# First unit of three attention layers: row maxima in twice as many parts, and a new merge order

## The chip, the cores and the metric

The kernel runs on one core of a Trainium2 chip. The metric is the device time of one execution, in microseconds (us); less is better. The core has a matrix engine (PE in the tables, TensorE), a vector engine (DVE, VectorE), an activation engine (ACT, ScalarE), a general engine (POOL, GpSimd) and SyncE (SP), which here only issues DMAs. Each runs its own instruction stream in order and waits for the others on semaphores.

## What is computed

Eight sequences of 128 tokens and 256 channels go through four layers. Each adds a gated cross attention and then a gated feed-forward block to x. The four attentions differ in heads and shapes, the softmax core is the same:

```
x = x + tanh(g_xattn[0]) * L0_xattn(layernorm(x), ctx)      # 16 heads of 8, 256 x 256 scores, per sequence
x = x + tanh(g_ffn[0])   * L0_ffn(layernorm(x))             # 8 experts, top 1 with capacity
x = x + tanh(g_xattn[1]) * L1_xattn(layernorm(x), ctx, ctx) # 8 heads of 16, 256 x 256 scores, per sequence
x = x + tanh(g_ffn[1])   * L1_ffn(layernorm(x))             # gate, up, down
x = x + tanh(g_xattn[2]) * L2_xattn(layernorm(x), ctx, mask)# 16 heads of 16, scores clipped at 50: no maxima
x = x + tanh(g_ffn[2])   * L2_ffn(layernorm(x))             # 16 experts, top 2, and a shared one
x = x + tanh(g_xattn[3]) * L3_xattn(layernorm(x), ctx)      # 16 heads of 16, all 1024 tokens against 1024 keys,
                                                            # q, k, v and the probabilities rounded to 8 bits
x = x + tanh(g_ffn[3])   * L3_ffn(layernorm(x))             # 4 experts, top 1

scores = q k^T * scale
attn = softmax(scores)          # exp(scores - row maximum) / sum
out = attn v
```

## The kernel before

The program is made in two steps. `plan()` writes one list of steps for the whole kernel; then each engine's program is that list walked from front to back, an engine emitting its own share of each step. So the order of the list is the order on every engine, the DMA queue of SyncE included.

An attention works in **units**: one sequence in the first three layers (8 units), two sequences (256 queries) in the last (4 units). A unit has these steps:

- the **front**: normalise, project (`fq`, `fk`), split fp32 into bf16 parts (`split`, on POOL), store them to DRAM (`store`) and load them back packed (`packs`);
- the **maxima tiles** (`smax`): PE makes scores of 128 queries in one PSUM bank (lines 1338 in the last layer, 1344 in the first two), DVE reduces each bank to row maxima (lines 1929 and 1933). A unit has 16 tiles in the first layer, 8 in the second, 64 in the last. They take turns in three banks (`psB`), which the projections and transposes use too;
- per **part** of the heads: the **negation** (`negsplit`, DVE lines 1943 to 1960: the maxima of the part are negated and split into two or three bf16 numbers), and the **turn** (`negmax`): PE transposes them (line 1354), ACT copies them out of PSUM (line 1659), and SyncE issues two or three DMAs that put them as extra rows under the queries (line 1180, `whole<-nmT`). With these rows a score matmul gives score minus maximum at once. The first two layers have one part a unit, the last has two;
- the **body**: for each group of 4 heads and each 128 keys a **score group** (`st`, 4 matmuls, line 1374), the exponential on ACT (line 1675), in the last layer a rounding on POOL (`round`, line 2342), and the **value group** (`pv`, lines 1406, or 1408 and 1418), one to three score groups later; after each group of heads `onorm` (line 1425, DVE lines 1976 and 1979). The first layer has 8 score groups a unit, the second 4, the last 32. The first score group of a part waits for that part's extra rows;
- the **end**: transposes, output projection, the update of x.

What sets the order is a merge: every stream of steps has a start and an end time in units, counted from the layer's start, and `merge` sorts all steps by them. The times stand in `TIMES`, one dict a layer. The body of a unit runs beside the maxima tiles of the next.

```
            if A.has_max:
                begin = u + at["max"] if u else at["max_first"]
                step = (u + at["max_end"] - begin) / A.parts
                for tiles, split, turn in maxes(units[u]):
                    begin += step
                    streams += [(tiles, begin - step, begin), ([split], begin, begin),
```

## Time and profile before

| | |
|---|---|
| median of 3 runs | 1189.02 us (1188.04 to 1189.3) |
| profiled execution, its own time | 1187.16 us |
| its span in the trace | 1185.4 us |
| busy share: PE, DVE, ACT, POOL | 80%, 56%, 37%, 32% |
| first layer's attention | about 8 to 185 us |
| second layer's attention | about 312 to 395 us |
| last layer's attention | about 714 to 1000 us |

The shares are means over stages of very different kind, so the argument goes by stretches. A row of the timeline tells the start, the duration, the engine and line, what is written and read, and how many instructions of that kind ran back to back; in square brackets how long the engine had been idle before, and who released it. A row of the windows tells the length of the stretch, the busy time of PE, PEld (weight loads), DVE, ACT and POOL in it with the number of instructions, and then the TensorE clock that was granted, where 1.00 is 2.4 GHz and 0.50 is 1.2 GHz, the DMA engines' share and GB/s.

### The profile page before, as it was taken

The page shows a single profiled execution, that of the slowest core. Times are in us where ns is not written, and L with a number is a line of the kernel's source. Part 1 is how long each engine was busy: PE and PEld are TensorE (multiplying, and loading weights), DVE is VectorE, ACT ScalarE, POOL GpSimd, SP SyncE. Part 2 cuts the span into 40 slices and gives each one's busy share as a digit, 9 for nine tenths or more (in the row PEclk, how much of TensorE's full clock was granted, in tenths as well). Part 3 has the DMA queues.
Part 4 walks back from the last instruction along what each step waited for, and adds up shares of the span by engine and source line. Part 5 has one row for each costly group of instructions (what it writes and reads, how often), then busy time and mean ns, then how long its engine had stood idle before and what let it go on. Part 6 is the DMA issues. An engine that isn't in the chain of part 4 may idle for free.

```text
span 1185.4 us, 18900 instructions
## 1 busy us (share of the span) xinstructions
PE 945.1 (80%) x6620; PEld 558.2 (47%) x6620; DVE 660.6 (56%) x1574; ACT 438.3 (37%) x722; POOL 383.5 (32%) x515
## 2 busy tenths in 40 slices
PE   3899985798299999777379726999989997199993
PEld 1455544687044456554247612344434444156662
DVE  5678753462679334777623358787887852211111
ACT  1366662111056313443014300466546575021220
POOL 5233204332631003442050061356555565200002
PEclk9999996989589999996589956699999999599997
DMA  6434524684543004542327530101210002700002
GB/s 183 122 102 146 175 82 186 187 291 153 125 113 83 1 1 121 173 95 67 142 102 227 170 95 15 41 2 42 108 42 2 2 3 108 267 21 23 14 14 80
DMA packets 112700, 116.32 MB, mean 98 GB/s; under 512 B 58824, under 2 KB 102408, under 8 KB 109576
## 3 DMA queue, kind: packets, MB, share of 16 engines
q1 hardware_dynamic: 101760, 96.62, 26.5%
q10 hardware_dynamic: 7776, 10.10, 2.6%
q0 software_dynamic: 3072, 8.39, 2.3%
q8 instruction: 56, 0.92, 0.3%
q14 instruction: 36, 0.29, 0.1%
HBM read 88.17 MB, written 30.67 MB: 100 GB/s over the span
## 4 chain that ended last, share of the span: by engine, by line
PE 47%; DVE 14%; DMA 7%; issue 7%; POOL 6%; ACT 2%; SPq 1%; POOLq 0%; ACTq 0%; DVEq 0%
PE psT L1523 7%; PE psT L1223 5%; PE psT L1374 5%; PE psB L1338 4%; DVE mxp L1929 4%; PE psB L1223 4%; PE psO L1418 3%; PE psB L1537 3%; PE psT L1486 2%; PE psB L1588 2%; PE psO L1408 2%; DMA scr_k_high<-sk 1%; PE psO L1406 1%; POOL scr_sorted L2354 1%; PE psB L1564 1%
## 5 line engine op out<-in xcount | busy, mean ns | idle before, releaser
L1929 DVE TENSOR_REDUCE mxp<-psB 128x1 f32<-128x512 f32 x256 | 163.7, 684 | 37.5 <-PE psB L1338 36.7
L1374 PE MATMUL psT<-whole 99*128 99x256 bf16 (+2 forms) x1024 | 153.1, 275 | 10.0 <-issue 9.0
L1933 DVE TENSOR_REDUCE mxp<-psB 128x2 f32<-128x512 f32 x192 | 123.5, 684 | 31.6 <-PE psB L1344 31.2
L1675 ACT ACTIVATE Pt<-psT,ln 128x1024 f32<-128x1024 f32 x96 | 106.7, 1114 | 63.8 <-PE psT L1374 62.7
L1374 PEld LDWEIGHTS psT<-whole 99*128 99x128 bf16 (+2 forms) x1024 | 96.5, 102 | 54.1 <-issue 21.5
L1675 ACT ACTIVATE Pt<-psT 128x1024 f32<-128x1024 f32 x96 | 98.1, 1024 | 58.3 <-PE psT L1374 56.6
L1338 PE MATMUL psB<-whole 96*128 96x512 bf16 x256 | 96.2, 427 | 24.3 <-DMA whole<-scr_q 13.9
L2283 POOL TENSOR_TENSOR rstd<-vare,cst 128x1 f32<-128x1 f32 x64 | 35.8, 562 | 231.3 <-DVE vare L1836 231.0
L1344 PE MATMUL psB<-whole 96*128 96x256 bf16 x384 | 78.0, 306 | 36.0 <-DMA whole<-scr_q 20.3
L1523 PE MATMUL psT<-whole,qf 128*128 x176 | 82.3, 612 | 0.6 <-ACT qf L1729 0.6
L2342 POOL TENSOR_SCALAR nb_t<-Pt 128x1024 f16<-128x1024 f32 x64 | 67.2, 1051 | 39.5 <-ACT Pt L1675 37.4
L2204 DVE TENSOR_TENSOR Pt<-psT,Pt 128x512 f32<-128x512 f32 x22 | 15.2, 691 | 100.3 <-ACT Pt L1735 100.3
L1344 PEld LDWEIGHTS psB<-whole 96*128 96x128 bf16 x384 | 30.7, 105 | 83.8 <-issue 34.8
L1406 PE MATMUL psO<-Pt,whole 128*32 128x256 f32 x768 | 62.9, 401 | 3.8 <-ACT Pt L1675 2.8
L1338 PEld LDWEIGHTS psB<-whole 96*128 96x128 bf16 x256 | 20.6, 100 | 89.2 <-issue 39.7
L1223 PE MATMUL psT<-xn_t,whole 128*128 128x512 f32 (+1 forms) x128 | 59.2, 614 | 0.0
L1418 PE MATMUL psO<-Pt,cst 128*32 128x256 f32 x768 | 59.2, 385 | 0.0
L2373 POOL DMA_INDIRECT xn_t<-scr_sorted_out,idx x8 | 7.7, 958 | 140.4 <-DMA scr_sorted_out<-xn 138.3
L1231 PE MATMUL psB<-cst,xn 128*128 128x128 f32 x96 | 23.3, 330 | 33.1 <-DVE xn L1769 32.2
L1523 PEld LDWEIGHTS psT<-whole,qf 128*128 128x128 f32 x176 | 32.8, 197 | 34.2 <-issue 34.2
L1425 PE MATMUL psB<-cst,Oe 128*128 128x128 f32 x160 | 37.8, 304 | 13.7 <-ACT Oe L1683 8.6
L1669 ACT ACTIVATE Pt<-nb_t,att_b,att 128x512 f32<-128x512 f32 x32 | 26.0, 813 | 48.9 <-DVEq L1969 48.6
(323 smaller groups left out, 1743.8 us busy)
## 6 DMA issues: line engine op xcount, KB each, us to landing
whole<-in_w SPq DMA_DIRECT2D x32, 512.0 KB, 5.2
whole<-in_w SPq DMA_DIRECT2D x5, 3072.0 KB, 10.3
xn<-scr_sorted ACTq DMA_DIRECT2D x42, 128.0 KB, 2.2
scr_q<-sq SPq DMA_DIRECT2D x48, 96.0 KB, 2.2
whole<-scr_q SPq DMA_DIRECT2D x24, 192.0 KB
whole<-scr_k SPq DMA_DIRECT2D x24, 192.0 KB, 3.5
scr_sorted_out<-xn SPq DMA_DIRECT2D x31, 128.0 KB, 2.4
scr_k<-sk SPq DMA_DIRECT2D x32, 96.0 KB, 1.9
```

The lines of the kernel that those rows point to most:

```text
L1223: ins = pe.matmul(dst, lhsT=lhs(kd), rhs=rhs(kd), start=(kd == 0), stop=(kd == halves - 1))
L1338: ins = pe.matmul(dst, lhsT=q_at[:, h * A.T + s.tc * P:h * A.T + (s.tc + 1) * P], rhs=k_at[:, h * NT + half * 512:h * NT + (half + 1) * 51 ...
L1344: ins = pe.matmul(dst[:, i * 256:(i + 1) * 256], lhsT=q_at[:, h * A.T + s.tc * P:h * A.T + (s.tc + 1) * P], rhs=k_at[:, h * A.T:(h + 1) * ...
L1374: ins = pe.matmul(psT[:, s.n % 2, i * A.T:(i + 1) * A.T], lhsT=k_at[:, h * kw + s.c * P:h * kw + (s.c + 1) * P], rhs=q_at[:, h * A.T:(h + ...
L1406: ins = pe.matmul(dst, lhsT=VA[:, u.g % 3, s.c * A.H + h, :], rhs=pr, start=first, stop=last)
L1418: ins = pe.matmul(dst, lhsT=const("sumsel"), rhs=pr, start=False, stop=last)
L1425: ins = pe.transpose(dst[:, tc * P:(tc + 1) * P], Oe[:, s.o % 2, tc * P:(tc + 1) * P], ident)
L1523: ins = pe.matmul(psT[:, s.n % 2, k * 512:(k + 1) * 512], lhsT=xeT[:, s.i % 2, kd, :], rhs=whole[:, bass.ds(s.un.k * SLOTW + at, 512)], st ...
L1675: act.activation(p_slot(A, s.p)[:, 0:4 * A.T], psT[:, s.n % 2, 0:4 * A.T], ACT.Exp, bias=bias, scale=scale).then_inc(T_used[s.n % 2], 1)
L1929: dve.tensor_reduce(mxp[:, s.un.g % 2, at:at + 1], psB[:, s.n % BANKS, :], AX.X, ALU.max).then_inc(bank_used[s.n % BANKS], 1)
L1933: dve.tensor_reduce(mxp[:, s.un.g % 2, at:at + 2], psB[:, s.n % BANKS, :].rearrange("p (h n) -> p h n", h=2), AX.X, ALU.max).then_inc(bank ...
L2342: pool.tensor_scalar(n_slot(s.p)[:, 0:w], p_slot(s.A, s.p)[:, 0:w], 1.0, OFFSET, ALU.mult, ALU.add).then_inc(rounded, 1)
```

## The change

It gives a unit its own number of parts: the first unit of each attention has 2 instead of 1 part (first and second layer) and 4 instead of 2 (last layer). The other units keep theirs. The times of the merge become separate for the first unit (`first_end`, `first_body`) and for the start of the second one's maxima (`max_second`), and the other times are new too. The first unit's body starts earlier in the order, while its later parts' maxima are still being made. No arithmetic changes but the order of the maxima tiles.

```diff
+FIRST_PARTS = (2, 2, 1, 4)
...
 TIMES = [
-    dict(front=0.339, store=0.638, packs=0.793, max=1.019, max_end=1.817, neg=1.926, body=2.312, end=3.927, start=0.17, span=1.026, max_first=1.418),
-    dict(front=0.315, store=0.667, packs=1.608, max=1.871, max_end=2.713, neg=2.846, body=3.334, end=5.364, start=0, span=0.958, max_first=2.13),
...
-    dict(front=0, fronts=[0.0, 0.005, 0.01, 0.02, 0.03, 0.04, 0.045, 0.045, 0.045, 0.045, 0.045, 0.058, 0.06, 0.079], rest=[0.0, 0.02, 0.06, 0.08, 0.11, 0.13, 0.15, 0.18, 0.21, 0.24, 0.27, 0.33, 0.34, 0.35], store=0.42, packs=0.43, max=0.909, max_end=1.919, neg=1.973, body=1.639, end=3.415, start=0, span=1.008, max_first=1.026)]
+    dict(front=0.327, store=0.638, packs=0.793, max=1.019, max_end=1.831, neg=2.01, body=2.312, end=3.957, start=0.17, span=1.026, max_first=1.484, first_end=2.214, first_body=2.177, max_second=1.253),
+    dict(front=0.315, store=0.667, packs=1.608, max=1.871, max_end=2.551, neg=2.846, body=3.334, end=5.364, start=0.047, span=0.911, max_first=2.13, first_end=2.545, first_body=3.087, max_second=1.871),
...
+    dict(front=0, fronts=[0.0, 0.005, 0.01, 0.02, 0.03, 0.04, 0.045, 0.045, 0.045, 0.045, 0.045, 0.058, 0.06, 0.079], rest=[0.0, 0.02, 0.06, 0.08, 0.11, 0.13, 0.15, 0.18, 0.21, 0.24, 0.27, 0.33, 0.34, 0.372], store=0.408, packs=0.43, max=0.942, max_end=1.936, neg=2.001, body=1.639, end=3.334, start=0, span=1.008, max_first=1.026, first_end=1.85, first_body=1.36, max_second=0.75)]
...
+            r.parts = FIRST_PARTS[A.layer] if u == 0 else A.parts
...
-                begin = u + at["max"] if u else at["max_first"]
-                step = (u + at["max_end"] - begin) / A.parts
+                begin = at["max_first"] if u == 0 else 1 + at["max_second"] if u == 1 else u + at["max"]
+                end = at["first_end"] if u == 0 else u + at["max_end"]
+                step = (end - begin) / units[u].parts
...
-            streams += [(body(units[u]), u + at["body"], body_end), (finish(units[u]), body_end + at["start"], u + at["end"]),
+            streams += [(body(units[u]), u + at["body"] if u else at["first_body"], body_end), (finish(units[u]), body_end + at["start"], u + at["end"]),
```

On PE at the head of the last layer's attention, from the middle of the first unit's maxima on (L1338 a maxima tile, L1354 the turn of a part, L1374 a score group), there stood before:

```order
L1338 MATMUL psB<-whole 128x512 x13
L1354 MATMUL psB<-ident,npt 24x128 x2
L1338 MATMUL psB<-whole 128x512 x9
L1374 MATMUL psT<-whole 128x256 x4
L1338 MATMUL psB<-whole 128x512 x2
L1374 MATMUL psT<-whole 128x256 x4
L1338 MATMUL psB<-whole 128x512 x2
L1374 MATMUL psT<-whole 128x256 x4
```

and now (the lines are three higher):

```order
L1341 MATMUL psB<-whole 128x512 x13
L1357 MATMUL psB<-ident,npt 12x128 x2
L1341 MATMUL psB<-whole 128x512 x3
L1278 MATMUL psB<-cst,tmp 128x128 x4
L1341 MATMUL psB<-whole 128x512 x3
L1377 MATMUL psT<-whole 128x256 x4
L1341 MATMUL psB<-whole 128x512 x3
L1377 MATMUL psT<-whole 128x256 x4
```

The first score group had 45 maxima tiles ahead of it and has 27; three instead of two tiles stand between score groups after it.

On PE in the second layer, from the last value group of a unit to the turn of the next but one, as it repeats from unit to unit (L1344 x2 is one maxima tile, L1231 a transpose for the feed-forward block, L1425 `onorm`, L1406 a value group), before:

```order
L1406 MATMUL psO<-Pt,whole 32x256 x4
L1231 MATMUL psB<-cst,xn 128x128 x2
L1344 MATMUL psB<-whole 128x256 x2
L1425 MATMUL psB<-cst,Oe 128x128 x2
L1344 MATMUL psB<-whole 128x256 x4
L1374 MATMUL psT<-whole 128x256 x4
L1344 MATMUL psB<-whole 128x256 x4
L1374 MATMUL psT<-whole 128x256 x4
L1406 MATMUL psO<-Pt,whole 32x256 x4
L1344 MATMUL psB<-whole 128x256 x2
L1374 MATMUL psT<-whole 128x256 x4
L1406 MATMUL psO<-Pt,whole 32x256 x4
```

and now:

```order
L1409 MATMUL psO<-Pt,whole 32x256 x4
L1234 MATMUL psB<-cst,xn 128x128 x2
L1347 MATMUL psB<-whole 128x256 x4
L1428 MATMUL psB<-cst,Oe 128x128 x2
L1347 MATMUL psB<-whole 128x256 x4
L1377 MATMUL psT<-whole 128x256 x4
L1347 MATMUL psB<-whole 128x256 x4
L1377 MATMUL psT<-whole 128x256 x4
L1409 MATMUL psO<-Pt,whole 32x256 x4
L1377 MATMUL psT<-whole 128x256 x4
L1409 MATMUL psO<-Pt,whole 32x256 x4
```

The tile that stood behind the first value group has moved ahead of the first score group, so that four tiles of that unit precede the score group instead of three.

On PE at the end of the first layer, around the turn of the last unit (L1354), before:

```order
L1406 MATMUL psO<-Pt,whole 32x256 x4
L1354 MATMUL psB<-ident,npt 32x128 x2
L1374 MATMUL psT<-whole 128x256 x4
L1406 MATMUL psO<-Pt,whole 32x256 x4
L1374 MATMUL psT<-whole 128x256 x4
```

and now:

```order
L1409 MATMUL psO<-Pt,whole 32x256 x4
L1377 MATMUL psT<-whole 128x256 x4
L1409 MATMUL psO<-Pt,whole 32x256 x4
L1357 MATMUL psB<-ident,npt 32x128 x2
L1377 MATMUL psT<-whole 128x256 x4
```

The turn comes one score group and one value group later.

## Rows read from the trace of the kernel before

**Rows 1.** The page's chain that ended last, share of the span by engine
```profile
PE 47%; DVE 14%; DMA 7%; issue 7%; POOL 6%; ACT 2%; SPq 1%; POOLq 0%; ACTq 0%; DVEq 0%
```

**Rows 2.** Windows of the last attention: length, busy time, clock, DMA share, GB/s
```profile
716.62:750.24 33.62, 27.33 (x61) 7.86 (x62) 31.25 (x59) 1.91 (x5) 3.70 (x5) 0.60 0.12 36
750.24:776.24 26.00, 25.88 (x225) 11.65 (x224) 19.52 (x37) 17.24 (x17) 13.59 (x13) 0.82 0.01 2
776.24:810.90 34.66, 31.85 (x338) 15.72 (x336) 28.38 (x52) 21.40 (x25) 21.64 (x21) 1.00 0.13 35
810.90:816.85 5.95, 5.79 (x63) 2.07 (x62) 5.32 (x9) 1.57 (x3) 2.09 (x2) 1.00 0.04 8
```

**Rows 3.** Timeline of DVE at the head of the last attention
```profile
737.08 5.47 DVE L1929 TENSOR_REDUCE mxp<-psB 128x1 f32<-128x512 f32 x9 [0.42 <-PE psB L1338]
742.58 0.18 DVE L1943 TENSOR_REDUCE nm<-mxp 128x16 f32<-128x32 f32 x1
...
743.52 8.06 DVE L1929 TENSOR_REDUCE mxp<-psB 128x1 f32<-128x512 f32 x13
```

**Rows 4.** Timeline of PE in the last attention
```profile
750.24 1.06 PE L1374 MATMUL psT<-whole 99*128 99x256 bf16 x4
751.09 1.06 PE L1338 MATMUL psB<-whole 96*128 96x512 bf16 x2
751.95 1.06 PE L1374 MATMUL psT<-whole 99*128 99x256 bf16 x4
...
758.53 1.00 PE L1374 MATMUL psT<-whole 99*128 99x256 bf16 x4
...
765.57 0.60 PE L1374 MATMUL psT<-whole 99*128 99x256 bf16 x4
...
767.20 0.60 PE L1374 MATMUL psT<-whole 99*128 99x256 bf16 x4
...
816.85 0.60 PE L1374 MATMUL psT<-whole 99*128 99x256 bf16 x4
```

**Rows 5.** Tile nm on DVE: duration in ns, least, median, greatest
```profile
L1952 DVE TENSOR_SCALAR npt<-nm x8: 174/186/823, 742.8 to 963.0; 128x16 bf16<-128x16 f32 x8
...
L1959 DVE CAST npt<-nm x8: 174/175/904, 743.2 to 963.6; 128x16 bf16<-128x16 f32 x8
```

**Rows 6.** Timeline of the second attention's repeating unit: PE, then DVE, then ACT
```profile
362.77 0.39 PE L1344 MATMUL psB<-whole 96*128 96x256 bf16 x2 [0.20 <-DVE mxp L1933]
363.00 0.60 PE L1374 MATMUL psT<-whole 98*128 98x256 bf16 x4
...
364.77 0.64 PE L1406 MATMUL psO<-Pt,whole 128*32 128x256 f32 x8
...
363.07 2.47 DVE L1933 TENSOR_REDUCE mxp<-psB 128x2 f32<-128x512 f32 x4
...
363.70 2.06 ACT L1675 ACTIVATE Pt<-psT 128x1024 f32<-128x1024 f32 x2 [1.65 <-PE psT L1374]
```

**Rows 7.** Timeline of the second attention's head: PE, then DVE
```profile
325.48 1.04 PE L1374 MATMUL psT<-whole 98*128 98x256 bf16 x4 [0.53 <-DMA whole<-nmT]
...
317.74 0.48 DVE L2220 SCALAR_TENSOR_TENSOR x<-xn_t,r,x 128x256 f32<-128x256 f32 x1 [0.27 <-DMA xn_t<-scr_expert_out,idx]
```

**Rows 8.** Timeline of the first attention's head: PE, then SP's queue
```profile
40.64 1.06 PE L1374 MATMUL psT<-whole 98*128 98x256 bf16 x4
...
55.00 0.38 PE L1344 MATMUL psB<-whole 96*128 96x256 bf16 x2 [3.25 <-issue]
...
45.31 0.89 SPq L1115 DMA_DIRECT2D scr_k<-sk  x2
```

**Rows 9.** Timeline of the first attention's end: PE, then SP's queue
```profile
160.84 0.28 PE L1354 MATMUL psB<-ident,npt 128*32 128x128 bf16 x2
...
165.44 0.60 PE L1374 MATMUL psT<-whole 98*128 98x256 bf16 x4
...
161.63 1.16 SPq L1180 DMA_DIRECT2D whole<-nmT  x2
```

More of the change, by code:

```diff
@@ L69, in __init__ @@
         self.b0 = b0
-        self.k_packed = self.k_packed_before = None
+        self.k_packed = self.k_packed_before = self.parts = None
 P = 128
@@ L145 @@
 TIMES = [
-    dict(front=0.339, store=0.638, packs=0.793, max=1.019, max_end=1.817, neg=1.926, body=2.312, end=3.927, start=0.17, span=1.026, max_first=1.418),
-    dict(front=0.315, store=0.667, packs=1.608, max=1.871, max_end=2.713, neg=2.846, body=3.334, end=5.364, start=0, span=0.958, max_first=2.13),
-    dict(front=0.368, fronts=[-0.15, 0.1, 0.278, 0.262, 0.45], store=0.58, packs=0.684, body=1.604, end=3.227, start=0.084, span=1.053),
-    dict(front=0, fronts=[0.0, 0.005, 0.01, 0.02, 0.03, 0.04, 0.045, 0.045, 0.045, 0.045, 0.045, 0.058, 0.06, 0.079], rest=[0.0, 0.02, 0.06, 0.08, 0.11, 0.13, 0.15, 0.18, 0.21, 0.24, 0.27, 0.33, 0.34, 0.35], store=0.42, packs=0.43, max=0.909, max_end=1.919, neg=1.973, body=1.639, end=3.415, start=0, span=1.008, max_first=1.026)]
+    dict(front=0.327, store=0.638, packs=0.793, max=1.019, max_end=1.831, neg=2.01, body=2.312, end=3.957, start=0.17, span=1.026, max_first=1.484, first_end=2.214, first_body=2.177, max_second=1.253),
+    dict(front=0.315, store=0.667, packs=1.608, max=1.871, max_end=2.551, neg=2.846, body=3.334, end=5.364, start=0.047, span=0.911, max_first=2.13, first_end=2.545, first_body=3.087, max_second=1.871),
+    dict(front=0.368, fronts=[-0.15, 0.1, 0.278, 0.262, 0.45], store=0.58, packs=0.684, body=1.604, end=3.227, start=0.084, span=1.053, first_body=1.604),
+    dict(front=0, fronts=[0.0, 0.005, 0.01, 0.02, 0.03, 0.04, 0.045, 0.045, 0.045, 0.045, 0.045, 0.058, 0.06, 0.079], rest=[0.0, 0.02, 0.06, 0.08, 0.11, 0.13, 0.15, 0.18, 0.21, 0.24, 0.27, 0.33, 0.34, 0.372], store=0.408, packs=0.43, max=0.942, max_end=1.936, neg=2.001, body=1.639, end=3.334, start=0, span=1.008, max_first=1.026, first_end=1.85, first_body=1.36, max_second=0.75)]
 def plan():
@@ L347, in maxes @@
             r.neg = []
-            per = A.H * A.NC * P // 512 // A.parts
-            for part in range(A.parts):
+            per = A.H * A.NC * P // 512 // r.parts
+            for part in range(r.parts):
                 tiles = []
@@ L375, in st @@
                 s = add("st", A=A, un=r, g=g, c=c, first=(i == 0), n=take("T"), p=take("P"))
-                if A.has_max and c == 0 and g % (A.G // A.parts) == 0:
-                    s.neg = r.neg[g * A.parts // A.G]
+                if A.has_max and c == 0 and g % (A.G // r.parts) == 0:
+                    s.neg = r.neg[g * r.parts // A.G]
                 s.clip = take("clip") if A.layer == 2 else None
@@ L1178, in _ @@
                         r = A.rows + p3
-                        HP = A.H // A.parts
+                        HP = A.H // s.un.parts
                         sp.dma_start(QP[r:r + 1, s.un.g % 3, s.j * HP * A.T:(s.j + 1) * HP * A.T],
@@ L1351, in _ @@
                     pe.wait_ge(neg_split, s.i + 1)
-                    w = A.lows * A.H // A.parts
+                    w = A.lows * A.H // s.un.parts
                     for tc in range(A.TC):
@@ L1657, in _ @@
                         act.wait_ge(neg_in[s.i % 2], neg_after[s.i - 2])
-                    w = A.lows * A.H // A.parts
+                    w = A.lows * A.H // s.un.parts
                     act.activation(nmT[0:w, s.i % 2, 0:A.T], m_slot(s.m).bitcast(BF16)[0:w, 0:A.T],
@@ L1936, in _ @@
                 elif s.kind == "negsplit":
-                    A, HP = s.A, s.A.H // s.A.parts
+                    A, HP = s.A, s.A.H // s.un.parts
                     w = A.TC * HP
                     turn(dve, bank_used, s.last_S)
-                    mx = mxp[:, s.un.g % 2, 0:w]
+                    src = mxp[:, s.un.g % 2, 0:A.TC * A.H].rearrange("p (t h) -> p t h", t=A.TC)[:, :, s.j * HP:(s.j + 1) * HP]
                     if A.layer == 3:
@@ L1944, in _ @@
                                                halves_[:, :, s.j * HP:(s.j + 1) * HP, :], AX.X, ALU.max))
-                        mx = nm[:, 1, 0:w]
+                        src = nm[:, 1, 0:w].rearrange("p (t h) -> p t h", t=A.TC)
                     if s.m_prev2 is not None:
@@ L1949, in _ @@
                     part = npt[:, s.i % 2, 0:A.lows * w].rearrange("p (t c h) -> p c t h", t=A.TC, c=A.lows)
-                    src = mx.rearrange("p (t h) -> p t h", t=A.TC)
                     left = nm[:, 0, 0:w].rearrange("p (t h) -> p t h", t=A.TC)
```

## The prediction

> **What bounds the kernel now.** I read the page's chain first: it runs 47% on TensorE, 14% on VectorE, 7% each on DMA and issue [rows 1]. So the kernel is bound by TensorE where it is dense and by somebody else at the heads of stages. Then the windows of the last attention, cut at its first maxima tile (716.62 us), its first score group (750.24), group 14 after it (776.24), the last of the first unit's groups that have maxima tiles between them (810.90), and the second unit's first score group (816.85). In the first window VectorE is busy 31.25 of 33.62 us and TensorE 27.33, at a granted clock of 0.60; in the second TensorE is busy 25.88 of 26.00; in the third 31.85 of 34.66, at clock 1.00, with VectorE at 28.38 [rows 2]. So ahead of the first score group VectorE's reductions set the time and everything that a score group feeds stands idle; behind it TensorE does. The change moves work over that border, in the one direction that can pay: TensorE's groups go into the stretch where it waits. For the other two attentions I read the timeline at the head, in one repeating unit and at the end.
>
> **Last attention, head.** A maxima tile costs VectorE 5.47 / 9 = 0.61 us [rows 3]. Of the first unit's tiles 45 preceded the first score group, now 27: 18 × 0.61 = 11.0 us earlier, at 739.3. Those 18 tiles aren't gone. From the first maxima tile to the second unit's first score group there were 111 tiles and are 113; I lay them out by the same three stretches. Groups 1 to 14 had 28 tiles beside them and have 43; the next 17 had 30 and have 33; the piece behind them had 8 and has 10 (less the groups, 45 + 28 + 30 + 8 before, 27 + 43 + 33 + 10 now).
>
> *Stretch two* becomes VectorE's: 43 × 0.61 = 26.2 us. Three negations lie in it. One costs 0.94 us when nothing disturbs it, from 742.58 to the next reduction at 743.52 [rows 3]. Its small instructions take 0.19 and 0.18 us in the median, but up to 0.82 and 0.90 [rows 5]; two such make 0.94 + 0.64 + 0.72 = 2.3. I take 1.3, nearer the undisturbed one because the medians are, so 3.9. The group's normalisation adds 0.5 (estimate, two small instructions beside those). While the clock is at 0.5 TensorE can be the later of the two: a score group then costs 0.85 (750.24 to 751.09) and a tile 0.43 (0.86 for two, to 751.95); four intervals with two tiles each, and one value group, took 8.29 [rows 4]. With 11 tiles instead of 8 and a turn that is 8.29 + 3 × 0.43 + about 0.2 to 0.4 = 9.7, against 11 × 0.61 + 1.0 = 7.7 on VectorE. Of these 2.0 us the three banks' backlog covers part; I add 1.0. Sum 26.2 + 3.9 + 0.5 + 1.0 = **31.6** (29.5 with negations at 0.94 and no wait; 35.9 with them at 2.3 and the wait at 2.0, and 0.3 more for the turn of each part) for 26.00 before.
>
> *Stretch three*: 34.66 before. Three more tiles cost VectorE 3 × 0.61 = 1.8, and TensorE 3 × 0.22 = 0.7 (half of the 0.43). TensorE was busy 31.85 there and VectorE 28.38 [rows 2]; both have room, so between nothing and 1.8; I take 1.3: **36.0**. *Tail*: 5.95 with VectorE busy 5.32 of it [rows 2]; two more tiles, 0.4 to 1.2: **6.5**.
>
> Sum 739.3 + 31.6 + 36.0 + 6.5 = 813.4 for 816.85 [rows 4], **-3.4 us**. Low end 739.3 + 29.5 + 34.7 + 6.4 = 809.9 (-6.9), high end 739.3 + 35.9 + 36.5 + 7.2 = 818.9 (+2.0). From the second unit on the order differs by single tiles, and TensorE is dense, so the shift reaches the end whole. I cost at nothing: two more turns there (two small transposes each, on TensorE under half a score group's 0.85 us [rows 4]), because VectorE is the later one; and SyncE's six more DMAs. Two such issues take 1.16 us [rows 9], so six are 3.5 us of a queue whose engines carry 1% in that stretch [rows 2]. If the second unit's loads, which stand ahead of the later parts' turns, came late, those 3.5 us would be added to the wait.
>
> The Trainium skill, "SBUF — State Buffer", section "Who interferes with whom", says that VectorE's copies, casts and scalar operations and GpSimd's work lock each other out for a whole instruction, while reductions don't take part. The trace agrees: the two forms of row 5 are the ones with the long maxima, 823 and 904 ns [rows 5]. By that rule a negation that falls beside roundings on GpSimd costs the 2.3 us of my upper bound; were all three to, the sum would be 3 us worse, +0.8 in all.
>
> **Second attention.** Head: the turns of both parts stand one behind the other and behind all 8 tiles of the unit, so little of the split can be used. VectorE besides waits until 317.74 for the combine of the layer before [rows 7]. The first score group comes at 325.48 behind its rows' DMA [rows 7]; it can be at most about 1.1 us earlier (two tiles' reductions of 0.6), but the second unit's maxima set the next step. Taken as **0** (-1.1 to 0.5). Repeating unit: the first score group (363.00) is released by reductions that take 2.47 / 4 = 0.62 us each [rows 6], and has one tile more ahead: +0.6. The tile no longer stands behind the first value group, so the later groups close up, but no nearer than ScalarE's exponential allows, 2.06 / 2 = 1.03 each, idle 1.65 us before the first [rows 6]: -0.35, half of a reduction. So +0.25 in each of the five intervals with this pattern, and -0.3 in the last one, where no tile is added ahead: **+1.0**. The ends are 0 (ScalarE's idle time hides all of it) and +2.0 (no closing up in three of the five).
>
> **First attention.** Head: the first body is dense from 40.64; the first wait is 3.25 us before 55.00, for the third unit's loads [rows 8]. They hang on the store at 45.31, and that on the projections of keys, which now have four reductions fewer ahead, up to 2.4 us. But the second part's row DMAs now stand in SyncE's queue ahead of that store, 1.16 us [rows 9] before its 0.89 [rows 8]. Half of what is left, **-0.7** (-1.6 to 0). End: the last unit's turn (160.84) moves behind one score group and one value group, 1.1 us; its rows are issued at 161.63 for 1.16 us and are needed at 165.44 [rows 9]. There the slack after issue is 2.65 us, which the landing mostly uses, as the 0.53 us wait for such rows elsewhere shows [rows 7]: **+0.9** (0 to +1.2). Together +0.2.
>
> **Sum.** -3.4 + 1.0 + 0.2 = -2.2 us. Against the profiled execution, 1187.16, this is 1185.0; against the median of 1189.02 it is **1186.8**. The profiled execution lies 1.9 us under that median, so I shift both alike. 0.2% is 2.4 us, about what a measurement of this kernel can tell from no change; the forecast lies just inside.
>
> **Rivals.**
> *VectorE never waits.* Negations run undisturbed, the half-clock stretch is covered, and the second attention's added tile hides in ScalarE's 1.65 us: -6.9 + 0 - 0.7 = -7.6, 1181.4. For it: VectorE was busy 31.25 of 33.62 us when it alone set the time [rows 2]. Against it: rows 5's maxima. 0.28.
> *The head's gain is given back.* VectorE becomes the bound of the whole first body, its added negations fall beside GpSimd's roundings, and score groups wait behind three tiles each at half clock: +2.0 + 1.0 + 0.2 = +3.2, 1192.2. Its place is stretch two; it decides once that stretch takes over 34 us (26.00 before, + 11.0 gained ahead, - 1.9 for the two stretches behind, - 1.2 for the other attentions). For it: GpSimd is busy 13.59 of 26.00 us there [rows 2], about half, so a negation often meets one. Against: the median is the undisturbed value. 0.15.
> *The clock doesn't rise.* TensorE ran at 0.60 while it waited for reductions and at 0.82 and 1.00 when dense [rows 2], and in the stretch it now waits again. A group with two tiles and a value group takes 767.20 - 765.57 = 1.63 us at full clock [rows 4], with a third tile 1.85, while VectorE sets 31.6 / 14 = 2.26. At half clock it is 0.85 + 3 × 0.43 and 1.2 for the value group (estimate: the 8.29 us of four intervals less 4 × 1.71 leaves 1.45 [rows 4], a wait included), 3.3. So every group that stays at half clock beyond my first four costs 1.0, two undo the forecast, and all ten make +10.4: -2.2 + 10.4 = +8.2, 1197.2. 0.07. [...]
>
> **How the numbers follow.** Forecast 0.50, of which 0.15 falls beyond 0.2% faster and 0.35 within; with 0.28 that is faster 0.43, same 0.35, and slower 0.15 + 0.07 = 0.22. The range reaches from the first rival's 1181.4 to the slower one's 1192.2; outside lie the clock rival and what overshoots the other ends.
>
> **What would show it.** The first score group of the last attention at about 22.7 us behind the first maxima tile instead of 33.6; 14 groups later VectorE busy over 90% of some 31 us, TensorE with short waits on reductions; the second unit's first score group 3 us nearer to the first maxima tile; a clock of 0.7 or more in stretch two. In the second attention each unit 0.25 us longer, in the first attention's end a wait of under 1 us for `nmT` rows. I am wrong if stretch two takes over 34 us, or if the shift is not there at the second unit's first group.

## The result, and the profile after

| | before | changed |
|---|---|---|
| median of 20 runs each | 1186.24 us (1182.36 to 1192.88) | 1179.07 us (1172.09 to 1188.04) |
| ratio | | 0.9941, 95% interval 0.9922 to 0.9959 |
| profiled execution, its own time | 1187.16 us | 1172.09 us |

The change makes the kernel 0.59% faster, some 7 us (0.41% to 0.78%), where I had forecast 2.2 us. The profiled execution of the changed kernel is the fastest of its 20, 7 us under their median, so the 15 us between the two profiles are not the effect. What can be compared are stretches that came out alike in many profiles. The table takes the starts of score groups from the timelines. Its "first maxima tile" is the tile's start on TensorE (714.02 us before, 706.99 now); the prediction and the windows below count from VectorE's first reduction of one, 2.6 to 2.7 us later (716.62 and 709.70). "Old" and "new" say whether the stretch has the order of before or of the change; the experiments below gave 14 more profiles. A value without a bracket is that of the two main profiles.

| stretch | old order | new order |
|---|---|---|
| start to last score group of first attention | 175.35 (174.23 to 176.59, 8 profiles) | 171.53 (171.53 to 174.88, 7 profiles) |
| second attention, second unit's first group to the last | 54.99 (54.36 to 55.22, 12 profiles) | 55.24 (55.23 to 55.24, 4 profiles) |
| last attention, first maxima tile to first group | 36.22 | 25.83 |
| 14 groups from there | 26.00 | 35.78 |
| 17 more | 34.66 | 34.73 |
| to the second unit's first group | 5.95 | 6.18 |
| second unit's body | 68.55 (68.54 to 68.61, 4 profiles) | 63.56 (63.56 to 63.58 in 3 profiles, 65.22 in a fourth) |
| third unit's body | 61.30 | 59.96 |
| fourth, to its last group | 46.38 | 46.93 |

The profiles counted for the first row have one order in the first attention. Stretches in between that no edit touches (the feed-forward blocks with their gathers, and the third attention) scatter by 1 to 7 us each between profiles, and 6.4 of the 15 us between the two main ones stand there.

The page's chain of the changed kernel, and the windows of its last attention; the first four rows stand for those of [rows 2]:

```profile
PE 48%; DVE 13%; DMA 7%; issue 6%; POOL 6%; ACT 2%; SPq 1%; POOLq 0%; ACTq 0%; DVEq 0%
```
```profile
709.70:732.82 23.12, 16.27 (x42) 5.75 (x43) 20.40 (x42) 1.91 (x5) 0.60 (x2) 0.65 0.00 1
732.82:768.60 35.78, 30.80 (x244) 12.74 (x243) 30.76 (x57) 17.67 (x18) 16.69 (x17) 0.86 0.12 35
768.60:803.33 34.73, 32.79 (x342) 16.07 (x341) 29.50 (x61) 21.59 (x25) 20.43 (x21) 1.00 0.01 1
803.33:809.51 6.18, 5.99 (x65) 2.14 (x64) 5.80 (x11) 1.55 (x3) 2.98 (x3) 1.00 0.65 179
809.51:873.07 63.56, 60.62 (x633) 29.56 (x631) 53.70 (x104) 39.67 (x45) 38.35 (x38) 1.00 0.21 72
873.07:933.03 59.96, 59.08 (x629) 28.57 (x628) 49.81 (x97) 38.85 (x43) 34.52 (x34) 1.00 0.01 2
```

The second unit's and the third unit's body of the kernel before, which the prediction didn't look at, and a piece out of the second unit's:

```profile
816.85:885.40 68.55, 62.62 (x633) 29.99 (x632) 56.58 (x106) 39.40 (x44) 38.41 (x38) 0.98 0.19 65
885.40:946.70 61.30, 59.19 (x629) 28.53 (x628) 48.86 (x97) 38.67 (x42) 34.57 (x34) 1.00 0.01 2
871.99:875.40 3.41, 3.41 (x26) 1.06 (x19) 1.56 (x3) 1.11 (x1) 2.85 (x4) 0.50 0.43 118
```

Three things are to be seen. The first score group comes 10.4 us nearer to the first maxima tile, and the next 14 groups take 9.8 us longer: of the head next to nothing stays. The second unit's body is 5.0 us shorter with as many instructions on TensorE (633); TensorE idled 68.55 - 62.62 = 5.9 us in it and idles 2.9. And the clock of that body went from 0.98 to 1.00. Before, it stood at 0.50 for 3.4 us from 871.99 on, which is some 1.7 us (half of 3.4, an estimate) of the 2.0 by which TensorE's busy time fell.

In the first 14 groups VectorE is busy 30.76 us, and I had summed 26.2 + 3.9 + 0.5 = 30.6. That it fits so well is partly luck: only two negations fall into this stretch, of 2.4 and 1.2 us (737.64 and 753.40), and the third comes at 769.09, behind its end. The other 5.0 us it waits for TensorE, for which I had set 1.0. The timelines of VectorE, of GpSimd and of TensorE show the place:

```profile
737.64 0.17 DVE L1946 TENSOR_REDUCE nm<-mxp 128x8 f32<-128x16 f32 x1
737.85 0.86 DVE L1954 TENSOR_SCALAR npt<-nm 128x8 bf16<-128x8 f32 x1
738.75 0.17 DVE L1959 SCALAR_TENSOR_TENSOR nm<-nm,npt 128x8 f32<-128x8 f32 x1
738.95 0.90 DVE L1961 CAST npt<-nm 128x8 bf16<-128x8 f32 x1
739.88 0.17 DVE L1962 TENSOR_TENSOR npt<-nm,npt 128x8 bf16<-128x8 f32 x1
...
743.94 0.69 DVE L1932 TENSOR_REDUCE mxp<-psB 128x1 f32<-128x512 f32 x1 [1.49 <-PE psB L1341]
...
746.94 3.73 DVE L1932 TENSOR_REDUCE mxp<-psB 128x1 f32<-128x512 f32 x6 [1.46 <-PE psB L1341]
```
```profile
737.64 2.18 POOL L2344 TENSOR_SCALAR nb_t<-Pt 128x1024 f16<-128x1024 f32 x2
```
```profile
740.71 0.61 PE L1341 MATMUL psB<-whole 96*128 96x512 bf16 x1 [2.65 <-DVE mxp L1932]
741.11 1.06 PE L1377 MATMUL psT<-whole 99*128 99x256 bf16 x4
...
744.54 1.06 PE L1377 MATMUL psT<-whole 99*128 99x256 bf16 x4
```

The windows on either side of the clock's fall:

```profile
736.00:739.40 3.40, 1.85 (x10) 0.67 (x7) 3.17 (x7) 2.38 (x3) 2.90 (x4) 1.00 0.40 118
739.40:746.20 6.80, 5.49 (x37) 2.06 (x37) 4.39 (x8) 1.99 (x3) 1.47 (x2) 0.50 0.38 116
```

The second part's negation meets two roundings and takes 2.4 us from its first instruction to the end of its last, instead of 1.0. TensorE's next tile needs a bank whose reduction stands behind this negation, so it waits 2.65 us. Within the wait its granted clock falls to 0.50, that is to 1.2 GHz, and stays there for 6.8 us (a score group takes 1.06 instead of 0.60). TensorE is now the later one itself, and VectorE waits twice 1.5 us. Each engine pays for the other's stall.

### The profile page after: what moved, and what is told of

The parts are those of the page before. It is cut to its first block, busy times and chain, and to the rows that moved or that the text cites. A ratio compares the mean times of both kernels' runs of the same rounds, so it can differ in the third digit from the quotient of the medians.

```text
span 1170.3 us, 18962 instructions
## 1 busy us (share of the span) xinstructions
PE 931.2 (80%) x6628; PEld 553.5 (47%) x6628; DVE 660.9 (56%) x1588; ACT 439.5 (38%) x726; POOL 382.9 (33%) x515
## 4 chain that ended last, share of the span: by engine, by line
PE 48%; DVE 13%; DMA 7%; issue 6%; POOL 6%; ACT 2%; SPq 1%; POOLq 0%; ACTq 0%; DVEq 0%
PE psT L1526 7%; PE psT L1226 6%; PE psT L1377 5%; PE psB L1341 4%; PE psB L1226 4%; PE psO L1421 4%; PE psB L1540 3%; DVE mxp L1932 3%; PE psT L1489 2%; PE psB L1591 2%; PE psO L1411 2%; PE psO L1409 1%; DVE mxp L1936 1%; POOL scr_sorted L2356 1%; PE psB L1567 1%
## 5 line engine op out<-in xcount | busy, mean ns | idle before, releaser
L1341 PE MATMUL psB<-whole 96*128 96x512 bf16 x256 | 90.1, 408 | 29.1 <-DVE mxp L1932 14.8
L1347 PE MATMUL psB<-whole 96*128 96x256 bf16 x384 | 75.4, 300 | 34.2 <-DMA whole<-scr_q 20.7
L1622 ACT ACTIVATE xn_t<-psB 128x256 f32<-128x256 f32 x48 | 18.2, 379 | 69.2 <-PE psB L1234 68.3
```

The lines of the kernel that those rows point to most:

```text
L1341: ins = pe.matmul(dst, lhsT=q_at[:, h * A.T + s.tc * P:h * A.T + (s.tc + 1) * P], rhs=k_at[:, h * NT + half * 512:h * NT + (half + 1) * 51 ...
L1347: ins = pe.matmul(dst[:, i * 256:(i + 1) * 256], lhsT=q_at[:, h * A.T + s.tc * P:h * A.T + (s.tc + 1) * P], rhs=k_at[:, h * A.T:(h + 1) * ...
```

## The experiments

All kernels are the changed one with some of its numbers put back. A layer "put back" has its old row of `TIMES`, with `first_end`, `first_body` and `max_second` equal to `max_end`, `body` and `max`, which gives the order of before. Ratios are to the kernel before; kernels without one had a single timed run.

**One layer at a time.**

```diff
-FIRST_PARTS = (2, 2, 1, 4)
+FIRST_PARTS = (2, 1, 1, 2)   # e1_l0: rows 2 and 4 of TIMES put back
+FIRST_PARTS = (1, 2, 1, 2)   # e2_l1: rows 1 and 4 put back
+FIRST_PARTS = (1, 1, 1, 4)   # e3_l3: rows 1 and 2 put back
```

> Only the first attention has the change; the other layers keep their old parts and times. If my prediction's working for this layer holds (head -0.7, end +0.9), the time is within 1 us of the kernel before. If the reading of the trace after holds (the third unit's loads land earlier, the wait of 3.25 us before its first maxima tile almost goes, and with it the drop of TensorE's clock behind it), this kernel is 3 to 4 us faster, and in the trace the third unit's first score group (index 8) comes 3 to 4 us earlier, and the last group of the layer still 3 to 4 us earlier.

Measured 0.9965 (0.9938 to 0.9992), some 4 us faster. Score group 8 stands at 57.64 instead of 61.70, the layer's last at 172.20 instead of 175.35. Groups are counted from 0 and a unit has eight, so group 8 is the second unit's first one, not the third's as the expectations for e1_l0 and e8_l0_head call it; the wait ahead of it is that for the third unit's loads.

> Only the second attention has the change. Prediction and the trace after agree: +0.2 us a unit, about +1 us in all between the second unit's first score group and the last one, -0.6 to -1 given back in the last unit; whole kernel 0 to 1.5 us slower. A rival is that the earlier first score group (split turn) pays 1 us and this layer is worth nothing.

Measured 0.9998 (0.9976 to 1.0019): nothing. From one unit's first group to the next it takes 8.97, 8.90, 8.89, 8.75 and 8.75 us instead of 8.52, 8.69, 8.69, 8.55 and 8.58, so +1.2 in five intervals, and 7.24 instead of 8.22 in the last one. The repeating unit, in the changed kernel, on TensorE and on ScalarE, for [rows 6]:

```profile
358.20 0.60 PE L1377 MATMUL psT<-whole 98*128 98x256 bf16 x4
...
359.98 0.64 PE L1409 MATMUL psO<-Pt,whole 128*32 128x256 f32 x8
```
```profile
358.90 2.06 ACT L1678 ACTIVATE Pt<-psT 128x1024 f32<-128x1024 f32 x2 [2.25 <-PE psT L1377]
```

The first value group still stands 1.8 us behind the first score group (1.77 before, 1.78 now), and ScalarE waits 2.25 instead of 1.65 us for that score group: the added tile is the 0.6 us.

> Only the last attention has the change. Prediction: first unit's head -3.4 us, nothing behind it. From the trace after: head -0.3 to -1 (half-clock stretch and negations beside GpSimd's rounding eat the 11 us), and 4 to 6 us in the second unit's body. If that second part was an accident of one execution, this kernel is only 0 to 2 us faster and its second body takes about 68 us as before; if it is due to the new order, the second body takes about 64 us and the kernel is 4 to 7 us faster.

Measured 0.9960 (0.9939 to 0.9982). The head takes 102.36 us to the second unit's first group (102.83 before), the second body 63.58: both as in the changed kernel, to 0.2 us. It was no accident.

**The last attention without the new first unit.**

```diff
-FIRST_PARTS = (2, 2, 1, 4)
+FIRST_PARTS = (1, 1, 1, 2)
-    first_end=1.85, first_body=1.36, max_second=0.75     # last row; rows 1 and 2 put back
+    first_end=1.919, first_body=1.639, max_second=0.909
```

> Only the last attention, and of it only the times that every unit uses (max, max_end, neg, store, end, rest); the first unit keeps two parts and its old head. If the gain in the second body comes from the steady order, it is here as well (second body 64 instead of 68 us, kernel 3 to 5 us faster). If the gain comes from the head, this kernel is within 1 us of the kernel before.

Measured 0.9964 (0.9938 to 0.9989), the same as e3_l3. The second body takes 64.90 us, the third 59.96, the fourth 46.91. From the first maxima tile to the layer's last group it is 272.96 us, with four parts in e3_l3 272.82. So nearly all of the last layer's gain is that of the times which all units share; the split of its first unit is worth 0.1 us in this pair. It has an effect in both directions: with it the second body is 1.3 us shorter (63.58), and the head 1.2 us longer (102.36 against 101.19).

**Which of these times.** Between the two bodies the traces differ at one conspicuous place. In the kernel before GpSimd's split of the next unit's queries (L2264 to L2267) stands in front of a rounding. The rounding ends at 871.51, and TensorE's value group starts at 871.61 after 1.78 us of idling; the row names no releaser, so that it waited for this rounding is inferred. Behind it TensorE runs slow. First GpSimd, then TensorE:

```profile
866.58 0.62 POOL L2264 TENSOR_SCALAR sq<-qf 128x512 bf16<-128x512 f32 x1
...
869.22 1.15 POOL L2267 TENSOR_TENSOR sq<-rem,sq 128x512 bf16<-128x512 f32 x1
870.47 1.04 POOL L2342 TENSOR_SCALAR nb_t<-Pt 128x1024 f16<-128x1024 f32 x1
```
```profile
871.61 0.29 PE L1408 MATMUL psO<-nb_t,whole 128*32 128x256 f16 x4 [1.78 <-issue]
...
872.88 1.06 PE L1374 MATMUL psT<-whole 99*128 99x256 bf16 x4
```

```diff
-    rest=[0.0, ..., 0.34, 0.35]     # last row as before, all rows put back
+    rest=[0.0, ..., 0.34, 0.372]    # e6_split: this alone
```

> The kernel before with one number changed: in the last layer the last entry of rest is 0.372 instead of 0.35. That moves one thing: in the second unit's body GpSimd's split of the queries (four instructions, 3.8 us) stands behind one more rounding; every other engine's order is the same. Theory: the split stood ahead of a rounding that TensorE's next value group needed; TensorE waited 1.8 us for it and then ran at half clock. Then the second body takes about 65 us instead of 68.6, and the whole kernel is 3 us faster. Rival: the gain in the second body comes from the maxima's new times (max, max_end, neg); then this kernel's second body still takes 68 us or more.

Measured 0.9983 (0.9964 to 1.0002), second body 68.38 us. My theory fell. The split now stands one rounding later, and a value group waits for the rounding behind it, with TensorE at half clock again (0.98 over the body, as before):

```profile
870.44 0.39 PE L1411 MATMUL psO<-whole 128*32 128x256 f16 x4 [1.56 <-POOL whole L2344]
```

> The last attention with the steady times of the change and the first unit's old head, as e4_l3_rest, but with the last entry of rest left at 0.35. If the place of the split is what counts, the second body takes 67 to 69 us here and the third stays at 60.0. If the maxima's times count, it takes about 65 us as in e4_l3_rest.

(e4_l3_rest with the last entry of `rest` at 0.35.) Second body 67.53, third 59.96, fourth 46.92 us, as expected if the split's place counts. Without the split's new place the second body gains 1.0, with it alone 0.2, with both 3.65: no sum of parts.

> The kernel before with two of the last layer's times changed: end 3.334 (a unit's finish and the next normalisation earlier) and the last entry of rest 0.372. My theory that the split's place alone makes the second body faster fell (68.4 us). New theory: GpSimd stands behind the normalisation's rstd, which waits for VectorE (3.99 us idle in the kernel before), and then meets the split; only both moved together help. Then the second body takes 65 to 66 us here. If the maxima's times are needed too, it stays at 67 us or more.

(The kernel before with `end` 3.334 and `rest` 0.372.) Second body 65.83, third 60.45 us.

> The kernel before with the last layer's max, max_end, neg and the last entry of rest changed, end left at 3.415. By the theory of rstd and split together the second body stays at 67 us or more; if the maxima's times and the split are what counts, it takes about 65 us as in e4_l3_rest. The third body's 1.34 us (61.30 to 59.96) and the fourth's loss of 0.54 us (46.38 to 46.92) are there if they come from the maxima's times, and not if they come from end.

(The kernel before with `max` 0.942, `max_end` 1.936, `neg` 2.001 and `rest` 0.372.) Second body 66.38, third 60.77, fourth 46.81 us. e11's body lies within the 65 to 66 us expected, but the theory behind it said that the maxima's times do nothing, and e12 lies between its two outcomes. With the split moved, either of the other two brings 2.0 to 2.6 us more than e6_split, and 0.85 (e11) or 0.53 us (e12) of the third body's 1.34. Neither `end` nor the maxima's times were changed alone, and `store` (0.42 to 0.408) in none of the pairs. The windows of the second body show what goes with its time:

| kernel | body, us | TensorE busy | idle | granted clock | longest wait |
|---|---|---|---|---|---|
| before | 68.55 | 62.62 | 5.9 | 0.98 | 1.78, value group |
| e6_split | 68.38 | 62.67 | 5.7 | 0.98 | 1.56, value group |
| e7_no_split | 67.53 | 63.24 | 4.3 | 0.97 | 1.54, tile |
| e12_max_split | 66.38 | 61.43 | 5.0 | 1.00 | 1.29, value group |
| e11_end_split | 65.83 | 62.42 | 3.4 | 1.00 | 0.86, tile |
| e4_l3_rest | 64.90 | 61.54 | 3.4 | 1.00 | 1.54, tile |
| changed | 63.56 | 60.62 | 2.9 | 1.00 | 1.54, tile |

The idle time falls from 5.9 to 2.9 us, and the three slowest are those whose clock fell. So what is shown is that the order does it, not which wait: that stays open. A wait of 1.54 us on a tile was followed by a slow score group in e7 and in e10 below, and not in e4 and the changed kernel, so its length alone doesn't decide. Why TensorE is busy for 62.42 us in e11 at full clock is open.

**The first attention's first unit alone.**

```diff
-TIMES[0]: max_first=1.418
+TIMES[0]: max_first=1.484, first_end=2.214, first_body=2.177, max_second=1.253   # e8_l0_head, 2 parts; all else put back
```

> Only the first attention, and of it only the first unit (two parts, max_first, first_end, first_body, max_second); the times that all units use stay old. If the first layer's gain comes from its head, the third unit's first score group is 3 to 4 us earlier than in the kernel before (61.7 to 62.1 us there, once 59.9), and the layer's last score group 4 us earlier. If it takes the moved fronts and turns as well, it is 1 to 2 us earlier only.

Group 8 at 59.97, last group at 173.29 us: 1.7 and 2.1 us earlier than in the kernel before, or 1.0 and 2.3 against the means of the eight old profiles (60.93 and 175.58). That is nearer to the second outcome. The head brings at least this part; whether the rest is the order or where the loads landed can't be told from one profile.

**What the collision of negation and rounding costs.** Two ways to rewrite VectorE's instructions in the last layer, with the same results (-2x + x is -x; `zero` is a bf16 tile of zeros):

```diff
-link(dve.tensor_scalar(part[:, 0], src, -1.0, None, ALU.mult))
+link(dve.scalar_tensor_tensor(out=part[:, 0], in0=src, scalar=-2.0, in1=src, op0=ALU.mult, op1=ALU.add))    # e9
+link(dve.scalar_tensor_tensor(out=part[:, 0], in0=src, scalar=-1.0, in1=zero, op0=ALU.mult, op1=ALU.add))   # e10
...
-link(dve.tensor_copy(part[:, 1], left))
+link(dve.scalar_tensor_tensor(out=part[:, 1], in0=left, scalar=1.0, in1=left, op0=ALU.mult, op1=ALU.max))   # e9
+link(dve.scalar_tensor_tensor(out=part[:, 1], in0=left, scalar=1.0, in1=zero, op0=ALU.mult, op1=ALU.add))   # e10
```

> The changed kernel, but the last layer's negation uses scalar_tensor_tensor for its first and fourth instruction instead of tensor_scalar and the cast; the numbers are the same. In the changed kernel these two took 0.86 and 0.90 us beside GpSimd's rounding in the second part's negation, and TensorE stood 2.65 us behind it and then ran at 1.2 GHz. If those two instructions wait for GpSimd because of their form, they take under 0.25 us now, the wait falls to about 1 us, and the second unit's first score group is 1.5 to 4 us earlier than in the changed kernel (102.4 us behind the first maxima tile there). If every VectorE instruction waits for GpSimd, nothing changes.

> The changed kernel, but the last layer's negation takes for its first and fourth instruction a scalar_tensor_tensor that adds a bf16 tile of zeros, so that one input is f32 and the other bf16, as in the second and fifth, which never took over 0.19 us. e9_neg_stt showed that scalar_tensor_tensor alone, with the same f32 tile as both inputs, waits like the cast (0.85 and 0.89 us). If the kinds of the inputs decide, all five take under 0.25 us, TensorE's wait of 2.65 us behind the second part's negation falls to about 1.2 us, and the second unit's first score group comes 1.5 to 4 us sooner than the 102.4 us behind the first maxima tile. If it is the place in the sequence (the first and fourth meet the roundings by chance of timing), two of the five stay at 0.85 us or more and nothing moves.

Measured 0.9939 (0.9912 to 0.9966) and 0.9951 (0.9928 to 0.9974), not to be told from the change; 102.34 and 102.24 us to the second unit's first group. In e9 the first and fourth instruction wait as before. In e10 it is the third and fifth, whose form was never touched:

```profile
738.31 0.17 DVE L1954 SCALAR_TENSOR_TENSOR npt<-nm,zero 128x8 bf16<-128x8 f32 x1
738.51 0.97 DVE L1959 SCALAR_TENSOR_TENSOR nm<-nm,npt 128x8 f32<-128x8 f32 x1
739.51 0.17 DVE L1961 SCALAR_TENSOR_TENSOR npt<-nm,zero 128x8 bf16<-128x8 f32 x1
739.72 0.89 DVE L1962 TENSOR_TENSOR npt<-nm,npt 128x8 bf16<-128x8 f32 x1
```
```profile
738.42 2.17 POOL L2344 TENSOR_SCALAR nb_t<-Pt 128x1024 f16<-128x1024 f32 x2
738.42 1.04 POOL L2344 TENSOR_SCALAR nb_t<-Pt 128x1024 f16<-128x1024 f32 x1
```

(The second of these rows is the first rounding alone.) In both kernels two of the five take 0.85 us or more and nothing moves, which is e10's second outcome. But which two is not fixed: neither the form nor the kinds of the inputs decide, since scalar_tensor_tensor and tensor_tensor wait too. Each of the two roundings catches one instruction until it ends (738.51 + 0.97 = 739.48, and the first rounding ends at 738.42 + 1.04 = 739.46). In the first unit of e15_l3_four_later below, where nothing rounds beside it, the same negation takes 1.0 us. The Trainium skill, "SBUF — State Buffer", section "Who interferes with whom", says that besides those with a two-port mode an instruction of VectorE with two inputs in SBUF contends with a GpSimd instruction that reads SBUF; the trace of e10 agrees (0.97 and 0.89 us). I had read only half of that rule into the prediction.

**Without the last layer's split, and two other heads for it.** All three have the first attention as in the change and the second put back.

```diff
-FIRST_PARTS = (2, 2, 1, 4)
+FIRST_PARTS = (2, 1, 1, 2)   # e13: last row as in e4_l3_rest
+FIRST_PARTS = (2, 1, 1, 2)   # e14: the same with first_body=1.55
+FIRST_PARTS = (2, 1, 1, 4)   # e15: last row of the change with first_body=1.45
```

> First attention as in the change, second attention old, last attention with the change's steady times but the first unit in two parts with its old head. If splitting the last layer's first unit into four parts is worth nothing in the end (the stage sums of e3_l3 and e4_l3_rest, 272.8 and 273.0 us from the first maxima tile to the last score group, say so), this kernel is as fast as the change or up to 1 us faster, 7 to 10 us faster than the kernel before. If the parts pay, it is 3 us slower than the change.

Measured 0.9944 (0.9922 to 0.9965): as fast as the change, with the new first unit in the first attention alone. From the first maxima tile of the last attention to its last group 274.72 us; the head took 102.90 here and 101.19 in e4_l3_rest, with one order. The 1.7 us go with the clock: behind the first score group TensorE ran at half clock for 3.2 us there and for 9.2 here.

> As e13_without_l3_parts (first attention changed, second old, last one with the steady times and two parts), but the first unit's body starts at 1.55 instead of 1.639: 39 maxima tiles instead of 45 ahead of the first score group, no negation added. If the extra negations and the clock behind them ate the gain, 2 to 3 of the 3.7 us by which the first group comes earlier stay: the second unit's first score group about 99.5 to 101 us behind the first maxima tile (101.2 and 102.9 in e4_l3_rest and e13_without_l3_parts). If VectorE's reductions as such set the time, it stays at 101 to 103.

Measured 0.9948 (0.9930 to 0.9965), 103.84 us to the second unit's first group. The first group could not start earlier, since its rows had not landed:

```profile
748.29 1.03 PE L1377 MATMUL psT<-whole 99*128 99x256 bf16 x4 [2.55 <-DMA whole<-nmT]
```

So this kernel couldn't answer what it was made for.

> As the change in the last attention (four parts), with the first attention changed and the second old, but the first unit's body starts at 1.45 instead of 1.36: 34 tiles instead of 27 ahead of the first score group, so that the second part's negation is finished before GpSimd's first rounding. If the collision and the clock are the cause, that negation takes about 1 us, TensorE's wait of 2.65 us is gone, and the second unit's first score group comes 1.5 to 3 us sooner than the 102.4 us of the change. If VectorE's reductions as such are, it stays at 102 to 103 us.

Measured 0.9941 (0.9917 to 0.9966). The second part's negation is now over before the first rounding, and TensorE no longer waits behind it (its longest wait after the first group is 0.79 us instead of 2.65):

```profile
740.78 0.17 DVE L1946 TENSOR_REDUCE nm<-mxp 128x8 f32<-128x16 f32 x1
740.99 0.17 DVE L1954 TENSOR_SCALAR npt<-nm 128x8 bf16<-128x8 f32 x1
...
741.60 0.17 DVE L1962 TENSOR_TENSOR npt<-nm,npt 128x8 bf16<-128x8 f32 x1
```

The second unit's first group comes after 101.91 us, 0.6 sooner than the 102.52 of the change, not 1.5 to 3. In exchange the first group had come 3.9 us later. The wait went, but the slow clock hardly did: behind the first group TensorE ran at half clock for 9.2 us, where the change has 10.0 (3.2 and 6.8).

```profile
740.61:749.78 9.17, 8.85 (x39) 3.60 (x37) 7.15 (x16) 5.82 (x6) 3.14 (x3) 0.50 0.48 130
```

e10_neg_mixed has the reverse, the collision and a wait of 2.75 us but only 4.5 us at half clock, and its head is 0.3 us shorter than that of the change. So neither alone accounts for what the head gives back. The whole time of e15_l3_four_later cannot be told from the change.

## Why the prediction was wrong

The sign and the second attention were right, the size was not: forecast 1186.8 with a range from 1181.4, measured 1179.07, or a gain of 7.2 us where 2.2 were forecast. (The kernel before came out at 1186.24 here, 2.8 us under the 1189.02 that the forecast started from, so the time missed by more than the gain did; as a gain, 7.2 lies just inside the 7.6 of the range's end.) The time came from places where I had set nothing or little, and not from the one I had set most on.

*Last attention, head, -3.4 forecast, -0.3 measured* (102.83 to 102.52). The 11.0 us earlier were right (10.4), stretch three and tail nearly so (34.73 and 6.18 for 36.0 and 6.5). The step that failed is stretch two, 35.78 us for 31.6, and in it the term "I add 1.0" for the time when TensorE is the later one: it was 5.0. The 35.9 of my upper bound had the pieces, a 2.3 us negation and TensorE late at half clock, but I added them as if they were independent. The trace shows them one behind the other: negation beside rounding 2.4 us, TensorE's wait of 2.65, half clock, then VectorE's waits. (A slip in the working: 8.29 + 3 × 0.43 + 0.2 to 0.4 is 9.8 to 10.0 and not 9.7, so the surplus that it names is 2.1 to 2.3 us and not 2.0; measured was more than twice that.) But the collision is not all. e15 takes it away and starts the first group 3.9 us later, and 0.6 us are gained, so most of what stretch two gives back it gives back in any case. Why the head comes out between 101.2 and 104.5 us in all sixteen profiles, whatever the order, is not settled: VectorE was busy 84.5 us of it before and 86.5 after (the sums of the windows from 716.62 and 709.70), TensorE 90.8 and 85.9, neither of them alone near the 100.

*"From the second unit on the order differs by single tiles, and TensorE is dense, so the shift reaches the end whole": -5.8 measured where 0 was set* (-5.0, -1.3 and +0.55 in the second, third and fourth body). This is the step that costs the most. I took the share of the whole for the state of the stretch: TensorE idled 5.9 us in the second body and ran part of it at half clock, and I had made no window there. One of the numbers of the diff (the last entry of `rest`) moves GpSimd's split behind a rounding, which I didn't price at all; neither did I `end`. Of the 5.0 us of the second body 3.65 come with the times that all units share (e4) and 1.3 with those of the first unit (63.58 in e3 against 64.90). e6 shows that the split's place alone does not do it (0.2), e7 that the other shared times without it bring 1.0. Which wait the others remove stays open.

*First attention, -0.7 and +0.9 forecast, -3.8 in the profile pair, -2.9 over the means* (175.6 for the eight profiles with the old order, 172.6 for the seven with the new one; e1_l0's ratio gives -4). The loads themselves did what the sum says: the projection of keys stands at 36.46 instead of 38.37, the row DMAs went in between, and the store came at 44.22 instead of 45.31 [rows 8], 1.1 us earlier; over the means the tile behind the wait started 0.8 us sooner (53.0 for 53.7), where -0.7 was forecast. (The row gives "issue" as the wait's end, so that it was the loads is inferred.) The term that failed is one that stood at nothing, the clock behind the wait. First the changed kernel, then the window from 57 to 60 us of the kernel before and that from 55 to 58 of the changed one:

```profile
52.56 0.38 PE L1347 MATMUL psB<-whole 96*128 96x256 bf16 x2 [0.59 <-issue]
...
55.88 0.60 PE L1303 MATMUL psB<-whole,w_at 128*128 128x256 f32 x2
```
```profile
57.00:60.00 3.00, 3.00 (x17) 1.40 (x16) 1.38 (x2) 0.70 (x2) 0.00 (x0) 0.56 0.00 0
```
```profile
55.00:58.00 3.00, 2.78 (x25) 1.61 (x24) 2.76 (x7) 1.33 (x3) 0.63 (x2) 1.00 0.57 178
```

The granted clock is 0.56 in the one and 1.00 in the other. In the eight profiles with the old order the wait was 2.39 to 3.27 us, and each time the clock fell, late in the wait or up to 1.2 us behind it. In those of the new one it was 0.55 to 0.89 us five times, the clock stayed at 1.00, and the layer's last group stood at 171.5 to 172.2; it was 1.67 and 1.69 us in e9 and e14, the clock fell, and the last group stood at 174.4 and 174.9. From the first maxima tile behind the wait to group 8, with the same 42 instructions on TensorE, it took 5.15 us in each of the five, 6.7 in e9 and e14, and 6.66 to 8.18 in the eight old ones. So the fallen clock cost 1.5 to 3.0 us on top of the wait, and 1.6 over the means (7.2 and 5.6). The wait itself became 1.9 us shorter over the means (2.8 and 1.0), 0.8 by the earlier loads and 1.1 because TensorE came to it later (52.0 for 50.9); no run tells which of the two keeps the clock up. At the end of the layer the late turn cost 0.26 us (165.44 - 162.16 = 3.28 before, 161.61 - 158.07 = 3.54 now, from the score group ahead to the last unit's first one [rows 9]), not 0.9; the row DMAs were issued at 159.14, 2.5 us ahead of the group at 161.61, and that was enough.

*Second attention, +1.0 forecast, 0 to +1 measured.* The repeating unit cost +1.2 in five intervals as forecast (+1.25); the last one gave back 1.0 instead of 0.3 (0.4 against e1_l0, where it took 7.63). The stretch row says +0.25 in the pair and +0.5 against the mean of the twelve old profiles (54.7), the ratio 0.9998.

*The parts together.* -0.3 - 5.8 - 2.9 + 0.5 is -8.5 us; the twenty runs of each kernel say -7.2, with an interval from -4.9 to -9.3. So the stretches account for the measured gain within its noise.

*The rivals.* "VectorE never waits" gave -7.6, nearest to the measured time, but by luck: its -6.9 in the head did not come. "The head's gain is given back" was right on its place (35.78 us, over the 34 that were to decide), its collision was there once in that size, and its total was wrong. "The clock doesn't rise" was wrong for the first body (0.86 granted in stretch two, 0.82 before) and yet pointed at the right quantity: short waits cost more than themselves, and removing them paid more. By the Trainium skill, "TensorE: Matmul & The Clock Gate", section "A second HAM failure mode: psum-queue depth-cycling", frequent short idling of TensorE between groups of matmuls makes its clock swing between the two levels. The traces agree in the swing, but here it went with single waits: in the stretches looked at the granted clock fell to 0.50 in or behind waits of 1.5 us or more, and came back each time.

## What to carry to other kernels

Price a reordering in every stretch that it touches, with a window for each, and look there for the later engine's idle time and for the granted clock; a stretch called dense from the page's shares hid 5.9 us of idle. Here a wait of TensorE cost itself and, where the clock fell, as much again (waits of 1.5 to 3.3 us, 1.5 to 3.0 us on top), so an edit that shortens such waits can be worth twice what the sum says. Starting the consumer of a split producer earlier need not pay: here the first group came 10 us earlier and the unit's head ended at the same time.

## What was not expected of the hardware

Instructions of VectorE with 8 elements a partition took 0.17 us alone and up to 0.97 beside a rounding on GpSimd, in every non-reducing form tried (tensor_scalar, cast, scalar_tensor_tensor, tensor_tensor), one for each rounding. One order gave, in different profiles, the same body to 0.05 us or one 1.7 us longer (63.56 and 65.22; the latter is e10_neg_mixed, which differs in the form of two instructions of a negation). TensorE's clock fell once there behind a wait of 1.5 us, and not in the others.
